# Twenty-four products without a reader, twelve in each of two pauses of TensorE, in a gated attention and mixture-of-experts layer

## The reference, cut to what matters

```python
x = x + tanh(g_xattn) * cross_attention(layernorm(x), ctx)    # x (2, 1024, 256), ctx (2, 154, 256), 16 heads
t = layernorm(x).reshape(2048, 256)
S = sigmoid(t @ Wg)                                           # 8 experts
G, I = top_k(S, 2)
h = gelu(einsum('nd,edf->enf', t, W1) + b1)                   # F = 1024
y = einsum('enf,efd->end', h, W2) + b2
x = x + tanh(g_ffn) * (G-weighted sum of the two chosen experts' rows of y)
```

## Time and profile before

| what | value |
|---|---|
| three runs | 476.35, 477.69, 482.83 us; median 477.69 |
| the profiled execution | 476.38 us, its span 474.6 us |
| mean granted TensorE clock | 0.933 of full |
| TensorE matmul busy | 402.5 us, 85% of the span |
| VectorE, ScalarE, GpSimd busy | 304.2, 226.8, 176.7 us |

### The profile page before, as it was taken

How to read it: one execution, slowest core, us unless ns; L and a number is a source line. 1 busy time by engine, 2 the same in 40 slices (tenths; PEclk the granted TensorE clock), 3 DMA queues, 4 the chain that set the end, 5 groups by cost and what they waited for, 6 DMA issues and landing times.

```text
span 474.6 us, 11156 instructions
## 1 busy us (share of the span) xinstructions
PE 402.5 (85%) x4056; PEld 318.9 (67%) x4056; DVE 304.2 (64%) x819; ACT 226.8 (48%) x577; POOL 176.7 (37%) x194
## 2 busy tenths in 40 slices
PE   5757988898989879872199999999999999999980
PEld 3632445455555445452189999999999999999970
DVE  4757787878877686867646656556555656565640
ACT  2343765655656557447054444444444444444420
POOL 8735532313222132110233444444444444444231
PEclk9965899999999999896579999999999999999996
DMA  7563444624554354312011223322222233332221
GB/s 220 111 177 112 122 141 127 218 97 120 153 155 121 100 178 123 106 45 49 19 42 35 48 47 56 56 51 47 48 46 48 47 50 53 54 49 42 33 24 22
DMA packets 35702, 40.25 MB, mean 85 GB/s; under 512 B 10982, under 2 KB 30306, under 8 KB 35650
## 3 DMA queue, kind: packets, MB, share of 16 engines
q0 software_dynamic: 12608, 27.48, 25.7%
q1 hardware_dynamic: 20497, 11.18, 8.5%
q10 hardware_dynamic: 2544, 0.88, 0.8%
HBM read 25.86 MB, written 9.50 MB: 75 GB/s over the span
## 4 chain that ended last, share of the span: by engine, by line
PE 65%; DVE 17%; DMA 7%; issue 4%; ACT 4%; POOL 2%; POOLq 0%; ACTq 0%; SPq 0%; DVEq 0%
PE bank L1318 7%; PE bank L1320 7%; PE bank L1319 7%; PE bank L1335 7%; PE bank L1334 7%; PE bank L1336 7%; PE bank L1063 4%; DMA out_rows<-y_sb,scatter_tab 4%; PE bank L1080 3%; DVE rowmax L734 3%; PE bank L1250 3%; PE bank L1101 3%; PE bank L1282 2%; DVE W L800 2%; PE bank L1223 1%
## 5 line engine op out<-in xcount | busy, mean ns | idle before, releaser
L1318 PE MATMUL bank<-xh,W 128*128 128x128 f16 x624 | 121.8, 221 | 0.9 <-DVE xl L975 0.9
L1319 PE MATMUL bank<-xl,W 128*128 128x128 f16 x624 | 121.8, 221 | 0.0
L1320 PE MATMUL bank<-xh,W 128*128 128x128 f16 x624 | 121.7, 221 | 0.0
L659 ACT ACTIVATE h<-bank,b1T 128x128 f32<-128x128 f32 x312 | 88.9, 368 | 62.3 <-PE bank L1320 59.7
L467 POOL DMA_INDIRECT out_rows<-y_sb,scatter_tab x39 | 61.8, 1585 | 112.7 <-DVE y_sb L993 103.7
L1334 PE MATMUL bank<-W,hh 128*128 x312 | 85.1, 273 | 1.0 <-DVE hl L986 1.0
L1336 PE MATMUL bank<-W,hl 128*128 x312 | 85.0, 273 | 0.0
L1335 PE MATMUL bank<-W,hh 128*128 x312 | 85.0, 273 | 0.0
L984 DVE CAST hh<-h 128x512 f16<-128x512 f32 x78 | 34.2, 439 | 63.5 <-ACT h L659 63.5
L734 DVE TENSOR_REDUCE rowmax<-bank 128x2 f32<-128x308 f32 x128 | 57.1, 471 | 25.8 <-PE bank L1080 24.7
L1318 PEld LDWEIGHTS bank<-xh,W 128*128 x624 | 61.7, 99 | 4.3 <-DVE xl L975 1.3
(11 more groups left out here) (185 smaller groups left out, 669.7 us busy)
## 6 DMA issues: line engine op xcount, KB each, us to landing
W_stage<-in_L_ffn_W POOLq DMA_DIRECT2D x32, 512.0 KB, 4.2
xn_scratch<-attn SPq DMA_DIRECT2D x8, 256.0 KB, 2.2
qst<-qh SPq DMA_DIRECT2D x60, 32.0 KB, 2.5
X_late<-in_x SPq DMA_DIRECT2D x6, 256.0 KB, 6.8
out_rows<-X_late SPq DMA_DIRECT2D x6, 256.0 KB, 2.5
qst<-ql SPq DMA_DIRECT2D x28, 32.0 KB, 2.8
xg<-xn_scratch,gather_tab POOLq DMA_INDIRECT x39, 2.9
out_rows<-y_sb,scatter_tab POOLq DMA_INDIRECT x39, 3.8
```

Source lines behind the costliest of these rows:

```text
L659: ins = nc.scalar.activation(h32[s % 4][:, m * P:(m + 1) * P], H_BANKS[s % 4][:, m * P:(m + 1) * P], ACT.Gelu_apprx_tanh, scale=1.0 / W_SC ...
L1318: nc.tensor.matmul(dst, wh, xh[t % 3][:, cut], start=(c == 0), stop=False)
L1319: nc.tensor.matmul(dst, wh, xl[t % 3][:, cut], start=False, stop=False)
L1320: ins = nc.tensor.matmul(dst, wl, xh[t % 3][:, cut], start=False, stop=(c == KC - 1))
```

## The change

A helper `keep_at_work(times)` issues so many identical products on TensorE. Each takes 128 by 128 f16 values of the first expert's stored first-layer weights as its stationary operand and 128 by 512 f16 values of the same weights as its moving operand, and writes all of bank 3, which nothing reads before it is written anew. The products wait for no semaphore and raise none. Twelve stand behind the counts of tiles 12 and 13 (fourteen tiles are counted then), and twelve behind the table products.

```diff
@@ -1110,6 +1110,10 @@
+            def keep_at_work(times):
+                for _ in range(times):
+                    nc.tensor.matmul(bank[3][:, :], W1[:, 0, 0, 0:2 * P].bitcast(F16), W1[:, 0, 0, 0:1024].bitcast(F16), start=True, stop=True)
@@ -1258,6 +1262,7 @@
                     if u == U and i == 6:
                         pe.wait_ge(chosen_made, 3)
                         count_places(NEXT)
+                        keep_at_work(12)
 
             pe.wait_ge(chosen_made, 4)
             count_places(LATE, last=True)
```

## The result

| kernel | runs | median | lowest to highest | ratio to before, 95% interval |
|---|---|---|---|---|
| before | 20 | 479.77 us | 476.35 to 482.83 | |
| changed | 20 | 477.06 us | 473.33 to 480.66 | 0.9948 (0.9925 to 0.9971) |

The change makes the kernel 0.5% faster, by 2.5 us (479.77 x 0.0052), with an interval of 1.4 to 3.6 us. The profiled execution of the changed kernel took 476.32 us (span 474.6), the one of before 476.38 (span 474.6): these two are equal. The gain has to be looked for inside.

What follows compares the result with a forecast made beforehand. TensorE's half clock behind two pauses was taken to bound the winnable time: 476.38 - 0 (products behind counts) - 1.7 (behind table products) = 474.7 us profiled, 475.3 as median; range over all cases roughly 473.2 to 477.9 us.

Steps and rivals of the forecast that it cites:

- The first series costs nothing: Twelve products behind the tile counts take 2.6 us, hidden with 3.9 us to spare before the transposes.
- It buys nothing: Products behind the tile counts gain 0, as the clock falls at 218.6 us, ahead of the transposes at 219.60.
- the logits' 0.82: Possible gain in routing logits if the clock stayed full: 1.04 in place of 1.86 us.
- The bounds 0 and 1.28: Limits in us on the gain from products behind the counts: transposes 0.46 plus logits 0.82 at most; 0 taken.
- The second series: Twelve products behind the table products raise the clock before layer 1, which starts 0.15 us earlier and runs at full clock.
- Late next is the low part of step 0: First layer 2 product waits 0.7 us for the gelu result's low part, limiting the gain to 1.7 us, not 2.4.
- Rival 4: No low-part wait appears before layer 2, so all 2.4 us come through; 474.0 to 474.6 us; chance 0.08.
- The sum: Whole kernel: 476.38 - 0 - 1.7 = 474.7 us on the profiled execution, 475.3 us as a median.
- the level: Starting time of the kernel before the change, taken as 477.0 us, the middle of four readings.
- the range that I gave the forecast itself: Whole-kernel time if the main forecast holds: 474.5 to 476.8 us; chance 0.60.
- the whole range: Kernel time over all cases, from roughly 473.2 to 477.9 us.
- rival 1: Clock rises too late behind the table products, layer 1 begins at half clock; 477.0 to 477.6 us; chance 0.17.

Runs made afterwards that it cites:

- first series alone: The changed kernel without the twelve products behind the table products; median 480.03 us, ratio 0.9994 to before.
- gelu early: The changed kernel plus a one-column gelu without a reader on ScalarE ahead of the expert stage, loading the table early; median 477.59 us, ratio 0.9946 to before.
- six: The changed kernel with 6 instead of 12 products behind the table products; median 480.12 us, ratio 0.9986 to before.
- frames: The changed kernel plus seven products without a reader in TensorE's pause in each of attention frames 1 to 7; median 477.88 us, ratio 0.9948 to before.
- setup, every product: The changed kernel plus 14 products ahead of the first maxima product and one behind each of 24 maxima products; median 475.15 us, ratio 0.9897 to before.
- second series alone: The changed kernel without the twelve products behind the tile counts; median 477.73 us, ratio 0.9963 to before.
- 29: The changed kernel with 29 instead of 12 products behind the tile counts; median 475.72 us, ratio 0.9933 to before.
- transfers spread: The changed kernel with 16 small bias transfers on SyncE's queue split four before unit 3's query, the rest later; median 474.72 us, ratio 0.9885 to before.
- 24: The changed kernel with 24 instead of 12 products behind the table products; median 480.00 us, ratio 1.0021 to before.

## Why the prediction was right

**The first series costs nothing.** Right: it ended 3.86 us ahead of the transposes. **It buys nothing.** Right for the changed kernel's trace and the mean of the first series alone (0.9994), not for every execution. I forecast the fall 2.9 us behind the last product; measured are 3.3 us (first alone), 3.8 (changed) and 4.4 (gelu early), and 3.3 to 5.1 over the nine traces with twelve. The delay that I took from the rows was shorter than any of these, and in the changed kernel's trace the fall came 0.06 us ahead of the transposes: that it bought exactly nothing there is luck. Of these nine, three have the transposes at 1.09 us (changed, first alone, six), two at 0.86 and 0.70 (frames; setup, every product), four at 0.63. The mean gain is (3 x 0 + 0.23 + 0.39 + 4 x 0.46) / 9 = 0.27 us, and none of the nine saved the logits' 0.82. The bounds 0 and 1.28 held; the value between them was a little too low. Twenty-nine products get all of it.

**The second series.** Right in mechanism and size: layer 1 starts 0.2 us nearer to the projection (0.15 forecast), and its way to the first layer 2 product is 5.53 us in place of 7.03 (5.5 forecast). I had it end 4.7 us behind its start, it took 4.66 to its successor (234.66 to 239.32); turn 0 was to take 0.39 and took 0.42. The moment of the rise scatters more than my two rows showed: 4.2 us behind the start in the changed kernel and with the second series alone, 1.9 with the gelu early, 1.6 with 29, 4.7 in the filled frames. A hardly minds: where the clock comes early, TensorE waits for the gather (1.01 us with the gelu early); where it comes late, the last products are a little late.

**Late next is the low part of step 0.** Right: the wait came, 0.54 us in place of my 0.7, and the gelu table taken out of the way ended it and gave 0.7 us. Rival 4 is excluded for this change; it comes true once the table load is out of the way, where the first layer 2 product waits for nothing.

**The sum.** 1.7 us forecast, 1.72 us in A, 2.5 us (1.4 to 3.6) by the runs. The step that was mis-sized is the level. I put the median of before at 477.0 from four readings; twenty gave 479.77. So 475.3 was 1.8 us too low although the gain was, if anything, larger. The measured 477.06 lies outside the range that I gave the forecast itself (474.5 to 476.8); only the upper end of the whole range, 477.9, took it in, and that end stood there for rival 1, which did not happen. The right gain on the right level, 479.77 - 1.7 = 478.1, would have been outside even that. That the time fell inside is luck: the level was 2.8 us too low, and by the medians the kernels differ by 2.7 us in place of 1.7. Where the rest of the runs' 2.5 us lies, behind 1.7 and the transposes' mean of 0.27, is within their interval and not shown.

**A reading.** The prediction has TensorE seven to nine tenths busy over the attention stage and nearly idle in slices 18 to 21. The slices say five in two of the first three, and only 19 and 20 are nearly idle. Nothing of the sum hangs on it.

**Rival 1** (the clock too late) did not come with twelve in any trace, though the filled frames came near: there the rise stood at 241.6, at the end of the series. With six its first half came true, half clock in layer 1, without the delay. The Trainium skill (TensorE: Matmul & The Clock Gate, Part 4: PE-mode transpose) says that the full clock doesn't engage for transposes. If that is to mean that they are no faster at it, as the prediction read it, 0.63 against 1.09 us on both sides of the change contradict it; whether transposes by themselves would raise the clock, no run here shows.

## What to carry to other kernels

A pause of TensorE that others end can be filled with products without a reader at little or no cost (none in the two pauses of the change, 0.85 us over six frames), but what that buys lies behind the pause: it pays where the filling reaches the end of the pause, and twelve that stop 3.9 us early are worth nearly nothing while twenty-nine are worth 1.3 us. A series that is too short (six) buys nothing, and one that is too long (24) gives back 1.5 us, so size it by the row of what ends the pause. Then look for what was hidden behind the slow clock: here a table load on another engine took 0.7 of 2.4 us, and one idle-time instruction gave it back in three traces, though too little for the runs of one kernel against another to tell.

## What was not expected of the hardware

The same pause of 1.59 us ahead of the turn at 74 us, in a part of TensorE's order that no edit here touches but that of the filled frames, kept full clock in the trace of before (1.99 us for the projection behind it) and lost it in the changed kernel's (3.31 us) and with the transfers spread (3.66 us). And 16 transfers of 0.5 KB took 10.06 us of issue on SyncE's queue, 0.63 each; the query queued behind them landed in time in three traces and up to 3.0 us late for TensorE in nine, as its last transfers took 1.9 to 2.5 or 3.4 to 4.0 us to land. Together the fall and the wait make one step of the attention differ by 4.7 us (20.84 to 25.55), nearly three times the 1.7 us that the change takes off A. Twenty executions of before differ by 6.5 us.
